# Two transfers for the query weights, and 13 instead of ten products of zeros, in a two-layer transformer kernel

## The reference

```python
h = _layernorm(x) * (1 + ca) + sa                     # 8 x 256 x 256
q = rms_norm((h @ Wq).reshape(Bx, Sx, 16, 128), gq)   # Wq: 256 x 2048, 16 heads
k = rms_norm((h @ Wk).reshape(Bx, Sx, 4, 128), gk)    # Wk: 256 x 512, 4 heads
v = (h @ Wv).reshape(Bx, Sx, 4, 128)
attn = softmax(where(causal, q @ k.T * 128 ** -0.5, -inf))
x = x + ga * ((attn @ v) @ Wo)
```

## Time and profile before

| | us |
|---|---|
| median of 3 runs | 1033.49 (1032.14 to 1033.54) |
| the profiled execution, its own time | 1035.23 |
| its span, first to last instruction | 1033.1 |
| TensorE busy | 966.9 (94%) |
| VectorE, ScalarE, GpSimd busy | 725.7, 673.3, 426.7 |
| mean granted TensorE clock | 0.978 of full |

### The profile page before, as it was taken

One profiled execution on the slowest core, in us unless ns is written; L12 is line 12 of the kernel. 1 busy time (PEld: TensorE's weight loads), 2 busy tenths in 40 slices (PEclk: granted clock), 3 DMA queues, 4 the chain that ended last, 5 costly groups with the idle time before them and its releaser, 6 DMA issues.

```text
span 1033.1 us, 20537 instructions
## 1 busy us (share of the span) xinstructions
PE 966.9 (94%) x6036; PEld 818.0 (79%) x6036; DVE 725.7 (70%) x2546; ACT 673.3 (65%) x1944; POOL 426.7 (41%) x447
## 2 busy tenths in 40 slices
PE   8999999999999999999999999996879889999980
PEld 5769878878988887887888788885767679999970
DVE  3564656787767687777669677865888678888870
ACT  2757767668677767768767875783746457777740
POOL 3322411421461362255146136323166646565662
PEclk9999999999999999999999999998999899999995
DMA  9927991993799420020012004237258788999954
GB/s 307 305 87 243 376 375 69 355 378 131 287 363 378 174 79 1 22 94 22 1 67 70 2 12 165 64 131 281 61 164 184 208 238 219 222 223 223 217 111 81
DMA packets 93677, 180.53 MB, mean 175 GB/s; under 512 B 9901, under 2 KB 29037, under 8 KB 92669
## 3 DMA queue, kind: packets, MB, share of 16 engines
q1 hardware_dynamic: 73467, 148.55, 43.2%
q0 software_dynamic: 18752, 30.30, 13.1%
q10 hardware_dynamic: 1346, 0.36, 0.2%
HBM read 77.71 MB, written 107.99 MB: 180 GB/s over the span
## 4 chain that ended last, share of the span: by engine, by line
PE 81%; DVE 7%; issue 4%; DMA 3%; ACT 1%; POOL 1%; another core or an unknown queue 1%; ACTq 1%; SPq 0%; DVEq 0%; POOLq 0%
PE bank L1112 12%; PE bank L1076 10%; PE bank L1048 10%; PE bank L1121 5%; PE bank L1066 5%; PE bank L1038 5%; PE bank L1027 4%; PE bank L998 3%; PE bank L1067 3%; PE bank L1057 2%; PE bank L1037 2%; PE bank L913 2%; PE bank L904 2%; PE bank L982 2%; PE bank L1020 2%
## 5 line engine op out<-in xcount | busy, mean ns | idle before, releaser
L1908 POOL TENSOR_TENSOR RB<-RB 128x512 f32<-128x512 f32 x64 | 66.7, 1042 | 277.1 <-DVE RB L1687 276.7
L1112 PE MATMUL bank<-RB 128*128 128x128 f32 x1264 | 157.3, 278 | 5.3 <-DVE BC L1801 2.3
L1112 PEld LDWEIGHTS bank<-RB 128*128 128x128 f32 x1264 | 150.4, 194 | 8.3 <-DVE BC L1801 3.4
L1377 ACT ACTIVATE RB<-RA,nw 128x512 f32 x158 | 105.4, 715 | 48.9 <-issue 22.3
L1076 PE MATMUL bank<-RA,RB 128*128 128x256 f32 x512 | 132.5, 381 | 1.1 <-ACT RB L1278 1.1
L1048 PE MATMUL bank<-RA 128*128 128x256 f32 x512 | 121.4, 380 | 0.3 <-DMA RA<-in_L_attn_Wq 0.3
L1048 PEld LDWEIGHTS bank<-RA 128*128 128x128 f32 x512 | 94.6, 190 | 15.6 <-issue 2.8
L1076 PEld LDWEIGHTS bank<-RA,RB 128*128 128x128 f32 x512 | 91.3, 190 | 14.4 <-issue 2.3
L1884 POOL TENSOR_TENSOR qs<-qs,half 128x4 f32<-128x4 f32 x64 | 65.6, 1024 | 63.8 <-DVE qs L1696 56.1
L1121 PE MATMUL bank<-RB,BC 128*128 128x256 f32 x316 | 83.1, 387 | 8.3 <-DVE BC L1814 7.3
L1278 ACT ACTIVATE RB<-bank 128x256 f32<-128x256 f32 x128 | 48.7, 381 | 45.8 <-PE bank L1067 43.9
(11 more groups left out here) (254 smaller groups left out, 2416.3 us busy)
## 6 DMA issues: line engine op xcount, KB each, us to landing
xsD<-BC SPq DMA_DIRECT2D x17, 4232.0 KB, 32.8
RB<-in_w2b SPq DMA_DIRECT2D x79, 256.0 KB
RB<-xsD SPq DMA_DIRECT2D x61, 264.5 KB
BC<-modD SPq DMA_DIRECT2D x16, 512.0 KB, 4.1
X<-xsD SPq DMA_DIRECT2D x18, 264.5 KB, 3.2
RA<-in_w SPq DMA_DIRECT2D x2, 2048.0 KB, 7.2
RA<-in_w SPq DMA_DIRECT2D x6, 512.0 KB, 8.6
RA<-in_L_attn_Wq SPq DMA_DIRECT2D x1, 2048.0 KB, 13.9
```

Source lines behind the costliest of these rows:

```text
L1112: m = pe.matmul(ps[:, 128 * j:128 * j + 128], WS[:, n % 2, c, 128 * j:128 * j + 128], XT[:, n % 2, c * 128:c * 128 + 128], start=(c == 0), ...
L1377: m = act.activation(WS[:, n % 2, c, :], W1[:, bass.ds(r, 1), c, :].rearrange("p a n -> p (a n)"), ACT.Copy, scale=nw[:, c:c + 1])
L1908: pool.tensor_tensor(sq, qrow, qrow, ALU.mult).then_inc(mine("q_sq", p), 1)
```

## The change

It does four things. The load of `Wq` becomes two transfers: columns 0 to 511 (the first four heads, 0.5 MB, semaphore `wq`) and columns 512 to 2047 (1.5 MB, `wq2`), in this order and in the same place of SyncE's queue; what waited for `wq` on SyncE now waits for `wq2`, and `q_mm(p)` waits for `wq2` as well from p = 2 on. The planner's table has `wq` at 12.5 instead of 17.0 and a new `wq2` at 16.5. TensorE's first products of zeros are 13 instead of ten. The six of `k_mm(0, 0)` go into that product's own bank, behind the wait for the bank's earlier holder, instead of into bank 7.

```diff
-LANDED = {..., "wv": 11.5, "wq": 17.0, "wo": 24.0, ...}
+LANDED = {..., "wv": 11.5, "wq": 12.5, "wq2": 16.5, "wo": 24.0, ...}
@@ queries()
-            bk = yield do("q_mm", n, first=True, leave=0, after=[("h_mod", 0, b), ("in", "wq")] + [("scores", 2 * n - 3)] * (n >= 2))
+            bk = yield do("q_mm", n, first=True, leave=0, after=[("h_mod", 0, b), ("in", "wq2" if n >= 2 else "wq")] + [("scores", 2 * n - 3)] * (n >= 2))
@@ sync
-            sp.dma_start(Wq, I["L0_attn_Wq"].rearrange("(c p) n -> p c n", c=2)).then_inc(L["wq"], 16)
+            wq_v = I["L0_attn_Wq"].rearrange("(c p) n -> p c n", c=2)
+            sp.dma_start(Wq[:, :, 0:512], wq_v[:, :, 0:512]).then_inc(L["wq"], 16)
+            sp.dma_start(Wq[:, :, 512:2048], wq_v[:, :, 512:2048]).then_inc(L["wq2"], 16)
...
-            on.wait_ge(L["wq"], 16)
+            on.wait_ge(L["wq2"], 16)
@@ tensor
-            def blanks(n):
+            def blanks(n, ps):
                 on.wait_ge(blank_set, 1)
                 for _ in range(n):
-                    pe.matmul(bank[7][:, :], blank[:, 0:128], blank, start=True, stop=True)
+                    pe.matmul(ps[:, :], blank[:, 0:128], blank, start=True, stop=True)
-            blanks(10)
+            blanks(13, bank[7])
@@ k_mm
                 ps = psum("k_mm", b, t)
+                clear("k_mm", b, t)
                 if (b, t) == (0, 0):
-                    blanks(6)
+                    blanks(6, ps)
                 on.wait_ge(*done("h_mod", 0, b))
                 on.wait_ge(L["wk"], 16)
-                clear("k_mm", b, t)
@@ q_mm
                 on.wait_ge(L["wq"], 16)
+                if p >= 2:
+                    on.wait_ge(L["wq2"], 16)
```

More of the change, by code:

```diff
@@ L64 @@
 HOP, LANDING = 0.2, {"bc": 5.0, "mod_store": 4.0, "clear": 14.0, "w12": 11.0, "xb": 3.2, "w2x": 3.5, "y_add": 4.0, "f_send": 3.0, "store": 4.0}
-LANDED = {"x0": 4.5, "cT": 4.0, "wmA": 6.0, "wk": 10.0, "wv": 11.5, "wq": 17.0, "wo": 24.0, "x": 30.0, "wmB": 45.0, "wm1": 50.0, "sw": 55.0, "small1": 55.0, "tables": 20.0, "w0": 60.0}
+LANDED = {"x0": 4.5, "cT": 4.0, "wmA": 6.0, "wk": 10.0, "wv": 11.5, "wq": 12.5, "wq2": 16.5, "wo": 24.0, "x": 30.0, "wmB": 45.0, "wm1": 50.0, "sw": 55.0, "small1": 55.0, "tables": 20.0, "w0": 60.0}
 class Once:
@@ L536, in build @@
         sems = {k: ctx.enter_context(nc.semaphore(f"{k[0]}_{k[1]}")) for k in plan.count}
-        LOADS = ("x0", "x1", "x2", "x3", "x4", "cT", "wmA", "wmB", "wm1", "ident", "wk", "wv", "wq", "wo", "gqk", "tables", "cb16", "sw", "small1", "bias", "w0")
+        LOADS = ("x0", "x1", "x2", "x3", "x4", "cT", "wmA", "wmB", "wm1", "ident", "wk", "wv", "wq", "wq2", "wo", "gqk", "tables", "cb16", "sw", "small1", "bias", "w0")
         L = {k: ctx.enter_context(nc.semaphore(f"in_{k}")) for k in LOADS}
```

## The result

The changed kernel takes **1055.62 us** (median of six runs, 1054.09 to 1058.34) against 1033.51 for the kernel before in the same session: a ratio of 1.0216, interval [1.0202, 1.0231]. That is 22 us slower, where 3.2 were forecast and 1040.5 was the end of the range. The direction was right and the size was not. The span of the profiled execution went from 1033.1 to 1052.6 us.

What follows compares the result with a forecast made beforehand. TensorE, busy 667.27 of 670 us from 30 to 700 us, was taken as the bound. Landing, zeros, clock and stalls put the reordered head at 34.9 against 31.64: 1033.49 + 3.2 = 1036.7 us, range 1032.0 to 1040.5.

Steps and rivals of the forecast that it cites:

- The order: TensorE's head: with wq at 12.5 the planner puts q_mm(0) ahead of every key and value.
- The first part of Wq: Start of the head's large products: the first quarter lands at 12.45, so they start there instead of 10.93, +1.52 us.
- The zeros on the path: Between q_mm(0) and k_mm(0,0): six zeros no longer fill a wait, +1.28 us at full clock, bound 2.56.
- The clock in q_mm(0): First large product: half of the half-clock penalty taken, +0.9 us; bounds 0 and 3.0, the latter with slow zeros.
- the half-clock case: At q_mm(0)'s start: TensorE, idle until 12.45, runs at 1.2 GHz, so the product takes 3.46 us instead of 1.73.
- New stalls: Head, TensorE waiting on VectorE before q_t(1), k_t(0,1) and scores(0): 0.35, 1.05 and 1.65, sum 3.05 us.
- The sum: Head up to p_t(0): 30.93 + 0.9 + 3.05 = 34.9 us, against a like point of 31.64 before.
- Ten to 13 zeros at 0: Start of the head: three more zeros end at 5.61, or 6.25 if slow, and cost 0 either way.
- carried through the full stretch: From 30 to 700 us: TensorE has no waits to give time back, so the head's +3.2 us arrives whole.
- Rival C: 700 to 860 us: shifted planner ties save TensorE idle time; a third, 9.4 us, gives 1027.3 us; chance 0.07.
- The sign of being wrong that it set: 700 to 860 us: the forecast is wrong if TensorE's idle time there differs by more than 2 us.

Runs made afterwards that it cites:

- changed_again: The changed kernel unedited, run again on another chip: 1.0167 of the kernel before, +17.1 us.
- head_old_rest_new: The changed kernel with the order of the kernel before up to scores(0) and the new order after it: 1.0088 of the kernel before, +9.0 us.
- new_to_wo127_rest_old: The changed kernel with its new order up to wo(127) and the order of the kernel before from there: 1.0129 of the kernel before, +13.2 us.
- head_new_rest_old: The changed kernel with its new order up to scores(0) and the order of the kernel before after it: 1.0070 of the kernel before, +7.2 us.
- old_order: The changed kernel with the planner's entry for wq back at 17.0, giving the order of the kernel before: 0.9985 of the kernel before, -1.5 us.
- order_alone: The kernel before with the planner's wq at 12.5 and the zeros of k_mm(0,0) in their own bank: 1.0211 of the kernel before, +21.6 us.
- zeros_ahead_of_q: The changed kernel with 11 zeros in front of q_mm(0) and none in front of k_mm(0,0): 1.0143 of the kernel before.

## Why the prediction was wrong

- **The order** [by the planner's rule, 12.75 + 0 against 12.75 + 0.04]: right, product by product down to p_t(0) and on VectorE.
- **The first part of Wq**, 12.45: its products start at 12.81, +0.36 (12.24 in changed_again).
- **The zeros on the path**, +1.28: 1.75 (16.36 to 18.11), partly at half clock.
- **The clock in q_mm(0)**, +0.9: 3.55 less 1.73 is +1.8, near the upper bound given. The text had called the half-clock case the likelier one and still taken half of it.
- **New stalls**, 3.05: starts 27.40, 28.35, 29.61 and 31.59 less 0.44 each leave 2.87 (0.51, 0.82 and 1.54). Right in sum.
- **Missing**: a second fall of the clock. The sum lists three stalls in a row, with only transposes between them, and prices only their length. It cost 3.1 us in this profile and 1.8 us in changed_again's (scores(0) at 31.73 to scores(2) at 36.55, less 3.03).
- **Ten to 13 zeros at 0**: right for this order. They ended at 6.72, past the bound of 6.25, because all of them ran at half clock's 0.427 us and not only the last three; that was hidden behind the wait for Wq.
- **The step that failed**: "Difference +3.2, carried through the full stretch", with all the reordering behind the head at zero. The head was mis-sized (8.2 instead of 3.2: clock +0.9 more, zeros +0.5, landing +0.4, second fall +3.1), and the larger part was not in the sum: the new order of the rest, +9.0 alone (head_old_rest_new), which the carry "through the full stretch" puts at nothing. Rival C had the place, 700 to 860 us, but only as a gain, and "it can as well cost" got no chance and no price. It also looked at idle time alone. The sign of being wrong that it set, idle time between 700 and 860 us off by more than 2 us, came with 6.2; but along the work, from the last `wo` to the end, idle time grew by 2.25 us and busy time, by more half clock, by 4.25. The range should have had C's mirror image in it.

**Left open.** The first chip shows 22 us and the third session's 17. From n_sel(1) to the end the new order takes 4.3 us more than the old one on the first chip (226.7 against 222.4) and 4.4 on the other (218.0 in changed_again against 213.6 in new_to_wo127_rest_old), so the difference is not made there; where it is made was not found. Nor was it found what in the first attention, between the head and wo(127), costs the 6 us by which new_to_wo127_rest_old lies above head_new_rest_old, on another chip and with about 2.5 us on either side of each; the planner's own times have 4.5 us more there. Nor do the three pieces fit exactly: 6 and 8.3 us would make 14 for all that lies behind the head, where head_old_rest_new measured 9.0. And no run holds the clock up between wo(127) and n_sel(1) in the new order, which would tell what the half clock does there.

## What to carry to other kernels

Where a planner writes the order, a number in its table is an edit of the whole program: before running, compare the two lists from end to end, print the planner's own finishing time for both, price the head and the rest as two changes, and give a reshuffled rest a cost side as wide as its gain side. A load that comes earlier should not be allowed to pull its consumer ahead of work whose inputs are there already; q_mm(0) in third place had its weights without any wait. When stalls are added up, ask of each group of them whether the clock survives it.

## What the runs showed of the hardware

The same 13 zeros at the head took between 4.49 and 5.73 us in nine profiles (5.73 in the changed kernel and old_order, 4.61 in changed_again, 4.49 in head_new_rest_old), and ten took 3.68 to 4.45 in five (before 3.77): the moment when the clock first rises is not tied to the program.

Nor is the second fall. Six profiles have the same list up to scores(0), but for the place of the zeros, and the same stalls of 0.35, 0.60 and 1.3 to 1.4 us in front of it, with transposes between. In three the clock then fell (changed kernel, 0.62 and 0.53 granted from 30 to 38 us; changed_again; head_new_rest_old), in three it stayed full (new_to_wo127_rest_old, order_alone, zeros_ahead_of_q), although new_to_wo127_rest_old has these stalls within 0.8 us of the place where changed_again has them. Windows of changed_again and new_to_wo127_rest_old:

```profile
31.00:34.00 3.00, 2.27 (x8) 2.00 (x9) 1.32 (x5) 0.00 (x0) 1.03 (x1) 0.64 1.08 302
31.00:34.00 3.00, 3.00 (x16) 2.72 (x17) 1.60 (x9) 1.32 (x7) 0.32 (x1) 1.00 1.07 291
```

That fits the Trainium skill's page "TensorE: Matmul & The Clock Gate", Part 1, which says that the gate's window runs free of the kernel.

And splitting a transfer did what arithmetic says: the first quarter of Wq was there at 12.67, the rest as before at 16.5.
